# Every piece of a gated recurrence at another gap of three hand-ordered engine programs (routed experts, then a scan over 256 steps, one core)

## What is computed

```python
x = x + (shared + routed) / 3        # shared = silu(x @ w1) * (x @ w3) @ w2; routed = the top two of 8 experts
def step(h, z_t):                    # h_0 = cond, z = the new x, 256 steps
    gate = sigmoid(h @ Wh.T + z_t @ Wz.T + b)
    h_new = tanh(h * (1 - alpha) + gate * z_t)
    return h_new, h_new
x = x + scan(step, cond, z)
```

## Time and profile before

| | us |
|---|---|
| median of 3 runs (833.88 to 836.47) | 834.77 |
| span of the profiled execution | 831.3 |
| tanh of the gate of step 0 starts | 200.3 |
| tanh of the gate of step 255 starts | 824.2 |
| busy: TensorE, VectorE, ScalarE, GpSimd | 729.4, 556.5, 474.7, 270.0 |

### The profile page before, as it was taken

How to read it: one execution, slowest core, us unless ns; L and a number is a source line. 1 busy time by engine, 2 the same in 40 slices (tenths; PEclk the granted TensorE clock), 3 DMA queues, 4 the chain that set the end, 5 groups by cost and what they waited for, 6 DMA issues and landing times.

```text
span 831.3 us, 23838 instructions
## 1 busy us (share of the span) xinstructions
PE 729.4 (88%) x8562; PEld 514.3 (62%) x8562; DVE 556.5 (67%) x2014; ACT 474.7 (57%) x1347; POOL 270.0 (32%) x284
## 2 busy tenths in 40 slices
PE   6899989789898989898989889998889999899653
PEld 4554677348786547787468775455788555586432
DVE  5877633296856696766678785877765577656643
ACT  5656555245667445676566665546756635666332
POOL 1057263275430445440271035651040371003000
PEclk9999999899999999999999999999999999999665
DMA  8748797846965556786769534445464371124000
GB/s 297 288 118 287 171 263 216 215 135 134 235 193 153 134 104 152 189 202 146 179 167 193 115 123 156 123 115 123 100 178 127 121 175 55 40 84 135 13 26 26
DMA packets 167106, 124.83 MB, mean 150 GB/s; under 512 B 119346, under 2 KB 147796, under 8 KB 166996
## 3 DMA queue, kind: packets, MB, share of 16 engines
q1 hardware_dynamic: 151076, 79.20, 40.0%
q0 software_dynamic: 14368, 41.96, 15.9%
q10 hardware_dynamic: 1552, 2.15, 0.7%
HBM read 39.90 MB, written 55.84 MB: 115 GB/s over the span
## 4 chain that ended last, share of the span: by engine, by line
PE 63%; DVE 17%; ACT 9%; DMA 5%; issue 4%; SPq 1%; POOL 0%; ACTq 0%; DVEq 0%; POOLq 0%
PE bank L1710 59%; DVE hid_low L1478 2%; PE bank L1909 2%; DVE pre L1532 2%; DVE taken L1529 2%; ACT th L1228 2%; ACT hs_high L1236 2%; DMA xe<-x_slots_even 1%; DVE o_ch L1552 1%; DVE left L1390 1%; PE bank L1844 1%; DVE x_parts L1349 1%; DVE full L1471 1%; SPq L915 1%; DMA xs<-x_parts 1%
## 5 line engine op out<-in xcount | busy, mean ns | idle before, releaser
L1710 PE MATMUL bank<-xe,w1e_high 128*128 128x128 f16 x1360 | 218.8, 222 | 6.8 <-DMA xe<-x_slots_even 3.5
L1710 PE MATMUL bank<-xs,w_high 128*128 128x512 f16 x512 | 169.3, 385 | 7.0 <-DVE w_low L1648 2.8
L1710 PE MATMUL bank<-xe,w1e_low 128*128 128x128 f16 x680 | 148.4, 221 | 0.0
L1478 DVE TENSOR_TENSOR hid_low<-full,hid_high 128x512 f16<-128x512 f32 (+1 forms) x152 | 103.2, 679 | 48.8 <-ACT hid_high L1181 36.8
L1710 PEld LDWEIGHTS bank<-xe,w1e_high 128*128 x1360 | 115.1, 98 | 26.1 <-issue 13.4
L1228 ACT ACTIVATE th<-bank 128x64 f32<-128x64 f32 x256 | 56.8, 222 | 129.4 <-PE bank L1710 126.2
L1529 DVE SCALAR_TENSOR_TENSOR taken<-th,zq 128x64 f32<-128x64 f32 x256 | 58.3, 228 | 99.1 <-ACT th L1228 95.7
L1710 PE MATMUL bank<-hs_high,gwt_high 128*128 128x32 f16 x1024 | 80.0, 180 | 48.3 <-ACT hs_high L1236 47.7
L1710 PEld LDWEIGHTS bank<-hs_high,gwt_high 128*128 128x128 f16 x1024 | 66.1, 98 | 85.9 <-ACT hs_high L1236 78.2
L1236 ACT ACTIVATE hs_high<-pre 128x64 f16<-128x64 f32 x256 | 65.2, 255 | 79.4 <-DVE pre L1532 70.9
L1049 POOL TENSOR_TENSOR fence_pool<-zero 128x1 f32<-128x1 f32 x12 | 2.8, 237 | 303.8 <-DMA y_slots_odd<-y_pair 93.6
(11 more groups left out here) (156 smaller groups left out, 1715.7 us busy)
## 6 DMA issues: line engine op xcount, KB each, us to landing
y_slots_even<-y_pair SPq DMA_DIRECT2D x45, 256.0 KB, 2.3
y_slots_odd<-y_pair SPq DMA_DIRECT2D x37, 256.0 KB, 2.2
x_res<-in_x_dram SPq DMA_DIRECT2D x16, 512.0 KB
out_dram<-o_tok SPq DMA_DIRECT2D x32, 256.0 KB, 3.0
x_tok<-in_x_dram SPq DMA_DIRECT2D x14, 512.0 KB, 5.1
x_slots_even<-zeros POOLq DMA_DIRECT2D x1, 4096.0 KB, 18.1
x_slots_odd<-zeros POOLq DMA_DIRECT2D x1, 4096.0 KB, 15.2
y_got<-in_L_cond_W1e_dram SPq DMA_DIRECT2D x4, 512.0 KB, 11.6
```

The source lines that it names most:

```text
L1478: dve.tensor_tensor(hid[1][:, u.i % NR, some], full32[:, u.i % 2, some], hid[0][:, u.i % NR, some], ALU.subtract).then_inc(s_lo, 1)
L1710: return pe.matmul(out_ap, w, mov, start=start, stop=stop, skip_group_check=True)
```

## The change

The three tables `PE_AT`, `ACT_AT` and `DVE_AT` are replaced. They hold the same pieces: 256 each of HIGH, STEP, GATE, STATE, MIX and REST, 64 fills, 32 splits of z on each of two engines. Nearly all of them stand at another gap: of the 256 STEPs 19 keep theirs, of the GATEs 30, of the 64 fills 7. Many fills now stand one at a time, with a HIGH or a STEP between the two of a chunk. `PE_AT` has 366 keys where it had 404, `ACT_AT` 382 where it had 293, `DVE_AT` 416 where it had 312. Nothing else is touched: the units, `OUT_AT`, `SCATTER_STEP`, `GATHER_STEP`, and the programs of SyncE and GpSimd are the same. From the diff, a place in the middle and the end of TensorE's table, and the end of ScalarE's and VectorE's:

```diff
@@ -110,353 +110,366 @@
 PE_AT = {
...
-    (43, 16): ((STEP, 3),), (44, 6): ((HIGH, 4),), (44, 8): ((STEP, 4),), (45, 9): ((HIGH, 5),),
-    (45, 10): ((STEP, 5),), (45, 13): ((HIGH, 6),),
-    (45, 14): ((STEP, 6), (HIGH, 7), (STEP, 7), (FILL, 4), (FILL, 5), (HIGH, 8), (STEP, 8),), (46, 5): ((HIGH, 9),),
...
-    (152, 6): ((HIGH, 230),), (152, 7): ((STEP, 230), (HIGH, 231),), (152, 8): ((STEP, 231), (HIGH, 232),),
-    (152, 9): ((STEP, 232), (HIGH, 233),), (153, 0): ((STEP, 233),),
-    (153, 5): ((HIGH, 234), (STEP, 234), (HIGH, 235),), (153, 6): ((STEP, 235),),
-    (153, 9): ((HIGH, 236), (STEP, 236), (FILL, 60), (FILL, 61), (HIGH, 237), (STEP, 237),),
-    (154, 1): ((HIGH, 238), (STEP, 238), (HIGH, 239), (STEP, 239), (FILL, 62), (FILL, 63), (HIGH, 240), (STEP, 240),),
...
+    (43, 5): ((HIGH, 2),), (43, 6): ((STEP, 2),), (43, 12): ((HIGH, 3), (STEP, 3),), (44, 4): ((HIGH, 4),),
+    (44, 5): ((STEP, 4),), (44, 10): ((HIGH, 5),), (44, 15): ((STEP, 5),), (45, 6): ((HIGH, 6), (STEP, 6),),
+    (45, 13): ((HIGH, 7), (STEP, 7),), (45, 14): ((FILL, 4), (HIGH, 8), (FILL, 5), (STEP, 8),),
...
+    (152, 5): ((HIGH, 233), (STEP, 233),), (152, 7): ((HIGH, 234), (STEP, 234), (HIGH, 235),), (152, 9): ((STEP, 235),),
+    (153, 5): ((HIGH, 236), (STEP, 236), (HIGH, 237),), (153, 6): ((STEP, 237),),
+    (153, 10): ((HIGH, 238), (STEP, 238), (HIGH, 239), (STEP, 239),), (153, 11): ((FILL, 60), (FILL, 61), (HIGH, 240),),
+    (154, 0): ((STEP, 240), (FILL, 62), (HIGH, 241), (STEP, 241),),
+    (154, 1): ((FILL, 63), (HIGH, 242), (STEP, 242), (HIGH, 243), (STEP, 243), (HIGH, 244), (STEP, 244), (HIGH, 245), (STEP, 245), (HIGH, 246), (STEP, 246), (HIGH, 247), (STEP, 247), (HIGH, 248), (STEP, 248),),
...
 ACT_AT = {
...
-    (154, 2): ((STATE, 234), (GATE, 235), (STATE, 235), (Z, 30), (Z, 31), (GATE, 236), (STATE, 236), (GATE, 237),),
...
+    (154, 4): ((STATE, 237), (Z, 30), (GATE, 238), (Z, 31), (STATE, 238), (GATE, 239), (STATE, 239), (GATE, 240), (STATE, 240), (GATE, 241), (STATE, 241), (GATE, 242),),
...
 DVE_AT = {
...
-    (153, 8): ((REST, 236), (MIX, 237), (REST, 237), (MIX, 238), (REST, 238), (MIX, 239), (REST, 239),),
...
+    (153, 7): ((MIX, 238), (Z, 30), (REST, 238), (Z, 31), (MIX, 239),), (153, 9): ((REST, 239), (MIX, 240),),
```

More of the change, by code:

```diff
@@ L119 @@
[L119 to L133, removed]
@@ new lines @@
+    (66, 14): ((FILL, 12), (FILL, 13), (HIGH, 47), (STEP, 47),), (67, 4): ((HIGH, 48), (STEP, 48),),
+    (67, 10): ((HIGH, 49),), (67, 11): ((STEP, 49),), (68, 4): ((HIGH, 50),), (68, 6): ((STEP, 50),),
+    (69, 1): ((HIGH, 51), (STEP, 51),), (69, 12): ((HIGH, 52), (STEP, 52), (FILL, 14),), (69, 13): ((FILL, 15),),
+    (69, 14): ((HIGH, 53), (STEP, 53),), (70, 5): ((HIGH, 54),), (70, 6): ((STEP, 54),), (70, 12): ((HIGH, 55),),
+    (70, 13): ((STEP, 55),), (71, 6): ((HIGH, 56), (STEP, 56),),
@@ new lines @@
+    (71, 12): ((HIGH, 57), (STEP, 57), (FILL, 16), (FILL, 17), (HIGH, 58), (STEP, 58),),
+    (72, 5): ((HIGH, 59), (STEP, 59),), (72, 11): ((HIGH, 60),), (72, 12): ((STEP, 60),),
+    (73, 5): ((HIGH, 61), (STEP, 61),), (73, 12): ((HIGH, 62),), (73, 15): ((STEP, 62),),
+    (74, 6): ((HIGH, 63), (STEP, 63),),
+    (74, 12): ((HIGH, 64), (STEP, 64), (FILL, 18), (FILL, 19), (HIGH, 65), (STEP, 65),),
+    (75, 5): ((HIGH, 66), (STEP, 66),), (75, 11): ((HIGH, 67), (STEP, 67),), (76, 5): ((HIGH, 68), (STEP, 68),),
@@ new lines @@
+    (109, 0): ((STEP, 143),), (109, 7): ((HIGH, 144), (STEP, 144),), (109, 14): ((HIGH, 145),),
+    (109, 15): ((STEP, 145), (FILL, 38), (FILL, 39),), (109, 16): ((HIGH, 146), (STEP, 146),),
+    (110, 1): ((HIGH, 147), (STEP, 147),), (110, 7): ((HIGH, 148), (STEP, 148),), (110, 17): ((HIGH, 149),),
+    (110, 18): ((STEP, 149),), (111, 6): ((HIGH, 150), (STEP, 150),), (111, 13): ((HIGH, 151), (STEP, 151),),
+    (112, 0): ((HIGH, 152),), (112, 4): ((STEP, 152),), (112, 18): ((HIGH, 153), (STEP, 153),),
@@ new lines @@
+    (113, 12): ((FILL, 40),), (113, 14): ((HIGH, 154), (FILL, 41),), (113, 18): ((STEP, 154),),
+    (114, 12): ((HIGH, 155), (STEP, 155),), (115, 3): ((HIGH, 156),), (115, 4): ((STEP, 156),),
+    (115, 10): ((HIGH, 157),), (115, 11): ((STEP, 157),), (116, 3): ((HIGH, 158),), (116, 4): ((STEP, 158),),
+    (116, 11): ((HIGH, 159), (STEP, 159),), (116, 12): ((FILL, 42),), (116, 14): ((HIGH, 160), (STEP, 160),),
+    (117, 6): ((HIGH, 161),), (117, 8): ((STEP, 161),), (118, 3): ((HIGH, 162), (STEP, 162),),
@@ new lines @@
+    (118, 10): ((HIGH, 163), (STEP, 163),), (119, 1): ((FILL, 43), (HIGH, 164), (STEP, 164),),
+    (119, 8): ((HIGH, 165), (STEP, 165),), (120, 0): ((HIGH, 166),), (120, 1): ((STEP, 166),),
+    (120, 8): ((HIGH, 167), (STEP, 167),), (120, 10): ((FILL, 44),), (120, 12): ((HIGH, 168), (STEP, 168),),
+    (120, 15): ((FILL, 45),), (121, 2): ((HIGH, 169), (STEP, 169),), (121, 9): ((HIGH, 170),),
+    (121, 10): ((STEP, 170),), (122, 3): ((HIGH, 171), (STEP, 171),), (122, 8): ((HIGH, 172), (STEP, 172),),
@@ new lines @@
+    (140, 9): ((HIGH, 205), (STEP, 205),), (140, 21): ((HIGH, 206),), (141, 1): ((STEP, 206),),
+    (141, 14): ((HIGH, 207),), (141, 15): ((STEP, 207),),
+    (141, 17): ((FILL, 52), (FILL, 53), (HIGH, 208), (STEP, 208), (FILL, 54), (FILL, 55), (HIGH, 209),),
+    (141, 18): ((STEP, 209),), (142, 4): ((HIGH, 210),), (142, 5): ((STEP, 210),),
+    (142, 11): ((HIGH, 211), (STEP, 211),), (143, 3): ((HIGH, 212),), (143, 4): ((STEP, 212),),
+    (143, 11): ((HIGH, 213), (STEP, 213),), (144, 5): ((HIGH, 214), (STEP, 214),),
```

632 lines of the change are left out of this document (314 added, 318 removed).

## The result

The changed kernel takes 780.73 us (median of 4 runs, 778.12 to 783.21) against 834.33 of the kernel before on the same chip (4 runs, 832.93 to 836.47): 0.9365 of its time, with a 95% interval of 0.9335 to 0.9395. That is 53.6 us less. Every line number of the old kernel stands 13 lines further down now (L1710 is L1723).

What follows compares the result with a forecast made beforehand. TensorE's program, with holes waiting for the recurrence's state, was taken to bound the long middle. 831.3 - 21.6 - 1.5 - 5.5 = 802.7 for the profiled execution, 806.5 us for the median of runs; range 795 to 824.

Steps and rivals of the forecast that it cites:

- TensorE's holes: Middle, steps 1 to 229: most of TensorE's waits for the recurrence's state go; gain 21.6 us, bounds 10 and 27.
- The sum: TensorE's middle: 1.12 us less the work ahead of each HIGH, over steps falling short; 22.5 us before, 1.6 after.
- the shortfalls: Per step on TensorE: work missing from 1.12 us between STEP s-1 and HIGH s, or from 0.20 before STEP.
- The tail: After the last z, with three more steps already done: -7.4, +0.8 for fills, +1.2 for z splits, taken as -5.5 us.
- ScalarE and VectorE: Pieces moved on these two engines, some ahead of a unit's first operation: no effect, ends -4 and +15 us.
- The slower rival: 62 more ScalarE and VectorE pieces ahead of units' first operations hold TensorE 0.7 us each: 850 us; chance 0.09.
- Half given back: Middle: TensorE's waits for units' results grow, giving back 10.8 us, plus a little of the tail: 820 us; chance 0.17.
- The clock rival: Seven 20 us windows of the middle regain full clock, up to 12.6 us more: 796 to 803; chance 0.15.
- The queues: SyncE and GpSimd: transfers follow units and steps and stay in time; nothing, or a few us of VectorE waiting.
- the shift of step 91: STEP 91 moves from (85, 19) to (86, 6); the transfer behind its gather goes from 428 to about 430, still in time.
- The signs: Trace: `hs_high` waits under 8 us, fewer 0.9 clock windows, tail about 33, tanh 47 later, tanh 255 some 28 sooner.
- the right case: The forecast holding, chance 0.45: waits for the state fall and the last z and last tanh come sooner.

Runs made afterwards that it cites:

- behind: Changed kernel with 56 pieces (34 on ScalarE, 22 on VectorE) moved from gap 0 of an expert unit to gap 1: 811.39 us.
- bare20: Changed kernel with HIGH and STEP of 20 steps, on TensorE alone, pulled up directly behind the STEP before: 806.18 us.
- fills: Changed kernel with the two fills of each of chunks 2 to 29 put together right ahead of the chunk's first HIGH: 802.78 us.
- coarse: Changed kernel with 275 pieces on ScalarE and 110 on VectorE drawn together at a few gaps of each unit: 847.88 us.
- ahead: Kernel before with 53 pieces on ScalarE and 119 on VectorE moved from gap 1 to gap 0 of expert units: 906.08 us.
- clock2: Kernel before with 200 added products with zeros ahead of 19 HIGHs, at most 0.8 us in one place: 831.80 us.
- clock_only: Kernel before with 337 added 128-column products with zeros ahead of 29 HIGHs, moving nothing: 833.61 us.
- tuned: Changed kernel with the 23 latest pieces moved one gap earlier on ScalarE (9) and VectorE (14): 782.46 us.

## Why the prediction was right or wrong

**The direction and TensorE's holes: right.** (The sum's price for a float32 transpose, 0.17 in its example of HIGH 7, is too high: the trace has 0.109. With that, the sums for the middle are 23.5 and 2.2 for HIGH where it has 22.5 and 1.6, which changes little.) The sum gave -21.6 and -1.5 for the middle from the work ahead of each HIGH. The wait for the state in the middle went from 29.4 to 7.3, -22.1, and under 8 was named as the sign. That it came true rests on the two other engines' tables too, as `behind` shows (below). `bare20` confirms the price by putting the holes back (25.5 us for 20; the shortfalls rise by 51.9 - 25.6 = 26.3), and `fills` by its waits.

**The tail: right, and 3 us short.** -5.5 was forecast, -8.4 came. The two terms put against it, +0.8 for the single fills and +1.2 for the splits of z between step 238's pieces, came to 0.2 together: from STEP 240 to HIGH 241 and from STEP 241 to HIGH 242 lie 1.29 and 1.17 us, where bare rounds have 1.12, and fill 60 started at once behind STEP 239 with z already split. That makes 7.5 us up to tanh 240; the other 0.9 came behind it, where round 249 takes 2.65 us before and 1.82 after.

**ScalarE and VectorE, "I take the change as nothing, with -4 and +15 as ends": wrong, and the step that failed.** The places of the pieces on these engines are worth as much as those on TensorE: 30.7 us for 56 of them one gap later, 67 for their fineness. And the holes of TensorE for units' results, which this term took as unchanged, fell by 12.5 us between units 42 and 133, at least 6.9 of them by the fineness of these tables (`coarse`), past the end of -4. The prediction took the way round these engines as a constant 1.12 us, and looked only at what a piece may hold up behind itself, never at what it stands behind. A piece that comes to its engine while a 0.6 or 0.7 us operation of a unit runs is late by up to that, one behind an operation that still waits by more, as the 2.07 against 0.29 us above. The lateness of the links of this chain (tanh behind STEP, `taken` behind the tanh, `hs_high` behind `pre`), summed over steps 1 to 239 of the trace wherever it is over 0.04 us, is 64.6 us before and 30.7 after, 60.1 in `behind` and 95.0 in `coarse`. Most of it is covered by TensorE's work. What isn't comes back first as waits for the state: between units 42 and 133, 28.0 us for `hs_high` and `hs_low` in `behind`, 49.0 in `coarse`, 6.9 in after, with the same order on TensorE, for which the prediction's shortfalls give 3.3 (over a longer stretch, steps 1 to 229). The lateness isn't a property of the two tables alone, though: `bare20` has them as changed, and the same sum is 53.4.

**The slower rival** had its mechanism right and its sign wrong for this table. The 62 more pieces ahead of the units' first operation are part of the gain, since they stand there where the input comes first: `behind` puts back 56 pieces of this kind. In the old TensorE order 172 such moves cost 71.6 us (`ahead`).

**Half given back: wrong.** It held that the units' results would become the next wait. TensorE's waits for them fell too, and ScalarE's waiting for VectorE ahead of `hid_high` of the shared units with them, by 10 us.

**The clock rival: right in kind.** It took up to 12.6 us for seven windows. Half-clock time between units 42 and 133 fell from 23.9 to 10.2 us, worth 4.7 by the starts and 4 (2 to 6) by `clock2`.

**The queues: nearly nothing, as said, with one exception.** VectorE waited 3.06 us for a gathered tile at unit 84, where the prediction saw the gathers in time. It is not the shift of step 91 that was looked at: the gathers there start when the stores of `y_pair` have landed, and that came only 16.3 us sooner than before (391.66 for 407.94), where unit 83 came 21.1 sooner (388.1 for 409.2). The fence on GpSimd, the gather behind it, and the wait on VectorE:

```profile
391.66 0.19 POOL L1062 TENSOR_TENSOR fence_pool<-zero 128x1 f32<-128x1 f32 x1 [30.10 <-DMA y_slots_even<-y_pair]
392.39 0.98 POOL L1121 DMA_INDIRECT y_got<-y_slots_even,where  x1 [0.54 <-issue]
...
396.99 0.48 DVE L1506 SCALAR_TENSOR_TENSOR r_part<-y_got,gate,x_res 128x256 f32<-128x256 f32 x1 [3.06 <-DMA y_got<-y_slots_even,where]
```

**The signs.** The waits for `hs_high` and the time from the last `zs_low` came as the right case named them, the latter stronger (30.1 for 33). Windows of 20 us at 0.9 fell from seven to three, though the page's coarser clock row doesn't show it. Step 47's tanh, said to be later than before, came at the same time (316.15 and 316.09). Step 255's came 53.9 us sooner, not 28. None of the signs was the lateness of a piece on ScalarE or VectorE, so they could come true with the sum short by half.

**What stays open.** By kind of hole, from unit 42 to the last z, the waits for `hs_high` fell by 26.6 us (35.5 to 8.9), those for units' results by 15.1 (18.4 to 3.3), and the lengthening at the half clock by 5.1; the tail is 8.4 more. These are amounts and not yet causes. For the state both are needed, the order on TensorE (`bare20`) and the places on the other two engines (`behind`), so its gain can't be divided between them. For the units' results `bare20` (2.3) and `fills` (4.1) rule out the bare rounds and the fills, `clock_only` (15.3) the clock, and `behind` (4.5) the 56 places. `coarse` (9.8) gives half of it to the fineness of the two tables. Whether the other half belongs to other lines of these tables or to the rest of TensorE's order isn't shown. Taking one engine's whole new table with the old ones of the other two, which would tell, isn't possible: in every such mixture the engines end up waiting for each other. `tuned` shows that what lateness is left in the changed kernel isn't won piece by piece: its 23 moves took nothing off the sum of it (33.6 against 30.7).

## What to carry to other kernels

Where several engines run programs ordered by hand, those orders are one object: price a new one by the whole round, and for each piece by what it stands behind on its engine as well as by what it holds. Count as cover only the work between a result's release and its use; spread long filler work, one piece at a time, over the rounds that have nothing else. And when a change rewrites three tables and the sum has a number from one, the other two want a range of their own, as wide as the sum of the lateness that the trace shows (64.6 us here), not from the waits that happen to be visible on the busiest engine. As a forecast of the time that sum is poor: `behind` has 60.1 and is 24 us faster than before, which has 64.6.

The Trainium skill's "Perfetto Trace Analysis", Identifying Performance Opportunities, says to improve the most contended engine first. I take that as TensorE here, at 88%; but the 30.7 us of `behind` lay in the order of two engines that are busy 57 and 67% of the span.
